# Two recurrent layers ordered one behind the other, and attention stacks written without DRAM

## The reference

```
x = x + attention(cond1(x, f, f))
x = x + ffn(cond2(x, f, f))

cond(r, k, v), for each channel c and batch:
  decay = exp(-exp(w[c])) * (0.5 + 0.5*tf[b]);  ek = exp(min(k,30));  ekv = ek*v
  (nf, df), (nb, db) = a[t] = a[t-1]*decay + (ekv, ek)[t], forward and backward in t
  euk = exp(min(u[c]+k, 30))
  num = nf + nb - ekv + euk*v;   den = df + db - ek + euk
  out = sigmoid(r) * num / max(den, 1e-8) * (0.8 + 0.2*tf[b])
```

## Time and profile before

| | before |
|---|---|
| time, median of 3 runs | 406.08 us (406.03 to 406.85) |
| the profiled execution | 407.77 us, span 405.9 us |
| PE busy | 317.9 us (78%) |
| DVE busy | 322.0 us (79%) |
| ACT busy | 201.4 us (50%) |
| POOL busy | 126.4 us (31%) |
| granted clock, mean | 0.898 of 2.4 GHz |
| data moved by DMA | 55.09 MB |

### The profile page before, as it was taken

How to read it: one execution, slowest core, us unless ns; L and a number is a source line. 1 busy time by engine, 2 the same in 40 slices (tenths; PEclk the granted TensorE clock), 3 DMA queues, 4 the chain that set the end, 5 groups by cost and what they waited for, 6 DMA issues and landing times.

```text
span 405.9 us, 6016 instructions
## 1 busy us (share of the span) xinstructions
PE 317.9 (78%) x1552; PEld 245.0 (60%) x1552; DVE 322.0 (79%) x625; ACT 201.4 (50%) x373; POOL 126.4 (31%) x116
## 2 busy tenths in 40 slices
PE   0042378378858887877897897999999999999994
PEld 0031256165737565555665675888888888888882
DVE  6989888966897475686567995888888988888883
ACT  4131406162625264366555564666666666666651
POOL 1519424162050001001222342334334334334331
PEclk9999559658965896896999998999999999999999
DMA  5965907801760176300543544556655566666531
GB/s 174 169 166 151 155 6 185 129 0 56 155 107 3 52 159 103 106 10 8 170 137 131 154 167 156 140 201 186 189 190 192 183 196 190 192 185 190 194 140 52
DMA packets 33055, 55.09 MB, mean 136 GB/s; under 512 B 5207, under 2 KB 13831, under 8 KB 32011
## 3 DMA queue, kind: packets, MB, share of 16 engines
q1 hardware_dynamic: 33034, 54.85, 50.4%
HBM read 47.55 MB, written 5.52 MB: 131 GB/s over the span
## 4 chain that ended last, share of the span: by engine, by line
PE 48%; DVE 13%; issue 3%; ACT 3%; DMA 2%; POOL 1%; DVEq 0%; SPq 0%; ACTq 0%
PE ps L1256 7%; PE ps L1258 7%; PE ps L1257 6%; PE ps L1267 6%; PE ps L1268 6%; PE ps L1269 6%; PE ps L1171 3%; DVE q_st L959 2%; DVE scan L1052 2%; DVE mx L806 2%; PE ps L1139 2%; DMA k_st<-qk_split 2%; DVE qk_lo L1057 1%; PE ps L1158 1%; PE ps L1128 1%
## 5 line engine op out<-in xcount | busy, mean ns | idle before, releaser
L457 POOL TENSOR_TENSOR scan<-scan 128x512 f32<-128x512 f32 x68 | 73.3, 1078 | 137.8 <-ACT scan L584 136.1
L1057 DVE TENSOR_TENSOR qk_lo<-scan,qk_hi 128x512 fp32r<-128x512 f32 x68 | 69.3, 1019 | 31.7 <-ACT qk_hi L591 31.7
L584 ACT ACTIVATE scan<-ps 128x512 f32<-128x512 f32 x68 | 40.7, 599 | 50.2 <-PE ps L1258 50.0
L1267 PE MATMUL ps<-qk_hi,k_st 128*128 128x512 f32 x136 | 54.5, 401 | 4.5 <-DVE qk_lo L1057 4.3
L1256 PE MATMUL ps<-hid_hi,k_st 128*128 128x512 f32 x136 | 54.6, 401 | 2.0 <-DVE q_st L959 2.0
L577 ACT ACTIVATE k_st<-clip 128x512 fp32r<-128x512 f32 x68 | 42.8, 631 | 24.8 <-PE ps L1269 24.8
L1139 PE MATMUL ps<-k_st,q_st 96*128 96x256 f32 x128 | 34.8, 395 | 25.9 <-DMA k_st<-qk_split 22.6
L1258 PE MATMUL ps<-hid_hi,q_st 128*128 128x512 f32 x136 | 54.1, 398 | 0.0
L1257 PE MATMUL ps<-hid_lo,k_st 128*128 128x512 f32 x136 | 53.9, 396 | 0.0
L1268 PE MATMUL ps<-qk_lo,k_st 128*128 128x512 f32 x136 | 53.5, 393 | 0.0
L1269 PE MATMUL ps<-qk_hi,q_st 128*128 128x512 f32 x136 | 53.5, 393 | 0.0
(11 more groups left out here) (118 smaller groups left out, 461.8 us busy)
## 6 DMA issues: line engine op xcount, KB each, us to landing
clip<-in_tiles SPq DMA_DIRECT2D x68, 256.0 KB, 3.0
ex<-gates SPq DMA_DIRECT2D x136, 128.0 KB, 2.9
q_st<-qk_split SPq DMA_DIRECT2D x16, 256.0 KB, 4.8
k_st<-qk_split SPq DMA_DIRECT2D x32, 128.0 KB, 5.6
qk_split<-qk_hi SPq DMA_DIRECT2D x8, 256.0 KB, 2.2
qk_split<-qk_lo SPq DMA_DIRECT2D x8, 256.0 KB, 2.2
f_sb<-in_fT SPq DMA_DIRECT2D x4, 256.0 KB, 10.5
x_sb<-in_xT SPq DMA_DIRECT2D x4, 256.0 KB, 9.7
```

Of the source, the lines that this page charges most:

```text
L457: g.tensor_tensor(sq[:, k], relu[:, k], relu[:, k], ALU.mult).then_inc(sq_ready, 1)
L1057: TT(act_lo[:, k], act[:, k], act_hi[:, k].bitcast(F32), ALU.subtract).then_inc(act_lo_ready, 1)
L1267: mm(acc, w_hi, act_hi[:, k], start=first, stop=False, skip_group_check=True)
```

## The change

Four things change together.

1. **Stacks.** `qk_dram` and `store_qk` go. `load_stack(b, half)` writes the stack of one half from `qk_hi` and `qk_lo` on chip, with 8 DMAs of 128 KB (16 rows of 8 KB in the stack out of 128 partitions of 1 KB), each pair waiting only for its half of q or k. `MAXROW` goes from 96 to 64: scores contract over 64 rows, shifted scores over 66, and no rows of zeros are filled. `evacuate_qk` waits for the stacks of the batch before to have landed, in place of the stores.
2. **Recurrences.** `scans`, `sums` and `num_den` are called for one layer and one of numerator and denominator at a time. Batch 0 works layer 1 up to hidden1 first, layer 2 between the projections; in the loop, layer 2 of batch b + 1 stands between the first maxima of batch b and layer 1 of batch b + 2 in its second part. For batch 0, POOL makes the sums of layer 2.
3. **Clips and exponentials.** Each exponential waits for its own clip, in the order f, f + u1, x, f + u2. `clips(b + 2)` stands behind the first 8 maxima of batch b, `exponentials(b + 2)` behind `evacuate_o(b - 1, 3)` and ahead of `evacuate_qk(b + 1, 0)`. `products` waits for one exponential at a time.
4. **Loads.** The two small loads `vec` and `cond` are issued by ACT. On SP the loads of x and f of batches 2 and 3, `wo`, `gw` and `gbb` move behind the first stacks; `bvb` behind batch 1. The projection of batch 0 waits for two of the three weight loads, `project_out` for the third. `unity` becomes part of `ones`.

```diff
-MAXROW = 96
+MAXROW = STACK
...
-            def load_stack(w, b, half):
+            def load_stack(b, half):
 
                 n = slot(b, half)
-                sp.wait_ge(st_qk[w], 32 * (b + 1))
                 if turn(b, half) > 1:
                     sp.wait_ge(t_ready, HB * (KC * b + half - SLOTS + 1))
-                src = qk_dram[w, b, half]
-                width = STACK // (2, 4)[w]
-                for r in range(0, STACK, width):
-                    rows = src.rearrange("n d s -> (n d) s") if w == 0 else src[r // (STACK // 2)]
-                    sp.dma_start((q_st, k_st)[w][r:r + width, n].rearrange("p h s -> p (h s)").bitcast(F32),
-                                 rows).then_inc(ld_stack[n], 16)
+                for w in range(2):
+                    for m, (part, ready) in enumerate(((qk_hi, qk_hi_ready), (qk_lo, qk_lo_ready))):
+                        sp.wait_ge(ready, 4 * b + 2 * w + half + 1)
+                        for role in ((m, m + 2), (2 * m, 2 * m + 1))[w]:
+                            sp.dma_start((q_st, k_st)[w][role * HD:(role + 1) * HD, n].bitcast(F32),
+                                         part[:, w, half].bitcast(F32)).then_inc(ld_stack[n], 16)
...
-            store_qk(0)
-            for half in range(KC):
-                for w in range(2):
-                    load_stack(w, 0, half)
+            load_stack(0, 0)
+            load_f(2)
+            load_x(2)
+            load_stack(0, 1)
+            sp.dma_start(wo[:], w_out).then_inc(ld_w, 16)
+            load_f(3)
+            load_x(3)
...
             products(0)
+            sums(0, 1, 1)
+            sums(0, 1, 0)
             products(1)
-            sums(1, 0, 4)
+            sums(1, 0, 1)
+            sums(1, 0, 0)
             add_logs1(1)
             for b in range(B):
+                if b + 1 < B:
+                    sums(b + 1, 1, 1)
+                    sums(b + 1, 1, 0)
                 if b + 2 < B:
                     products(b + 2)
-                    sums(b + 2, 0, 2)
+                    sums(b + 2, 0, 1)
                 if b > 0:
                     add_logs2(b - 1)
                 if b + 2 < B:
-                    sums(b + 2, 2, 4)
+                    sums(b + 2, 0, 0)
...
-                for n in range(4):
+                for i, n in enumerate((0, 1, 3, 2)):
+                    sc.wait_ge(clip_ready, 6 * b + (1, 3, 4, 6)[i])
                     a.activation(ex[:, n], clip[:, n], ACT.Exp, scale=1.0 if n < 3 else -1.0).then_inc(ex_ready, 1)
...
                     evacuate_o(b - 1, 3)
+                if b + 2 < B:
+                    exponentials(b + 2)
                 if b + 1 < B:
                     evacuate_qk(b + 1, 0)
...
-                if b + 3 < B:
-                    exponentials(b + 3)
...
-            scans(0, 0, 0, 4)
-            scans(0, 1, 0, 4)
-            scans(0, 0, 4, 8)
+            scans(0, 0, 1, 0)
+            scans(0, 0, 1, 1)
             first_sums(1)
-            num_den(0, 1)
-            scans(0, 1, 4, 8)
+            scans(0, 0, 0, 0)
+            num_den(0, 0, 1)
+            scans(0, 0, 0, 1)
             first_sums(0)
-            num_den(0, 0)
+            num_den(0, 0, 0)
             first_logs()
             hidden1(0)
+            scans(0, 1, 1, 0)
+            scans(0, 1, 1, 1)
+            dve.wait_ge(ld_w, 32)
+            split_qk(0, 0)
+            scans(0, 1, 0, 0)
+            split_qk(0, 1)
+            scans(0, 1, 0, 1)
+            num_den(0, 1, 1)
+            num_den(0, 1, 0)
             clips(1)
-            scans(1, 0, 0, 8)
-            dve.wait_ge(ld_w, 48)
-            split_qk(0, 0)
-            scans(1, 1, 0, 4)
-            split_qk(0, 1)
-            scans(1, 1, 4, 8)
             add_v_bias(0)
-            num_den(1, 1)
-            clips(2)
-            num_den(1, 0)
+            scans(1, 0, 1, 0)
+            scans(1, 0, 1, 1)
+            scans(1, 0, 0, 0)
+            scans(1, 0, 0, 1)
+            num_den(1, 0, 1)
+            num_den(1, 0, 0)
...
                 for h in range(HB):
                     maximum(b, h)
                     next(route_last, None)
+                    if nxt and h < 4:
+                        scans(b + 1, 1, 1 - h // 2, h % 2)
+                    if nxt and h == 4:
+                        num_den(b + 1, 1, 1)
                     if nxt and h == 5:
                         hidden1(b + 1)
+                    if nxt and h == 6:
+                        num_den(b + 1, 1, 0)
+                if nxt2:
+                    clips(b + 2)
                 low_max(b, 0)
...
                 if nxt2:
-                    scans(b + 2, 1, 0, 6)
+                    num_den(b + 2, 0, 1)
+                    scans(b + 2, 0, 0, 1)
                 if b > 0:
                     hidden2(b - 1)
                 if nxt2:
-                    scans(b + 2, 1, 6, 8)
-                    num_den(b + 2, 1)
-                    num_den(b + 2, 0)
-                if b + 3 < B:
-                    clips(b + 3)
+                    num_den(b + 2, 0, 0)
```

More of the change, by code:

```diff
@@ L264, in _, with load_f, load_x @@
         def _(sp):
-            sp.dma_start(vec[:], vecs).then_inc(ld_vec, 16)
-            sp.dma_start(cond_sb[:], cond.partition_broadcast(P)).then_inc(ld_vec, 16)
-            for b in range(B):
+            def load_f(b):
                 sp.dma_start(f_sb[:, :, tok(b)], fT[:, :, tok(b)]).then_inc(ld_f[b], 16)
+            def load_x(b):
                 sp.dma_start(x_sb[:, :, tok(b)], xT[:, :, tok(b)]).then_inc(ld_x[b], 16)
[L270 to L282, removed]
+            load_f(0)
+            load_x(0)
+            sp.dma_start(wi[:], w_in).then_inc(ld_w, 16)
+            load_f(1)
+            load_x(1)
+            sp.dma_start(bvb[:], bv.partition_broadcast(P)).then_inc(ld_w, 16)
+            sp.wait_ge(ones_ready, 1)
+            sp.dma_start(k_st[MAXROW:MAXROW + 2].rearrange("p n h s -> p (n h) s").bitcast(F32),
+                         ones[0:2].unsqueeze(1).broadcast_to([2, SLOTS * HB, S])).then_inc(ld_ones, 16)
             def load_raw(t, k):
@@ L342, in _ @@
                 if b + 1 < B:
-                    store_qk(b + 1)
-                    for w in range(2):
-                        load_stack(w, b + 1, 0)
+                    load_stack(b + 1, 0)
                 if b + 1 == B:
@@ L353, in _ @@
                 if b + 1 < B:
-                    for w in range(2):
-                        load_stack(w, b + 1, 1)
-            sp.wait_ge(st_unity, 16)
+                    load_stack(b + 1, 1)
+            sp.wait_ge(st_ones, 16)
             sp.wait_ge(lnsum1_ready, B)
@@ L399, in products, with sums @@
                 pool.wait_ge(ld_f[b], 16)
-                pool.wait_ge(ex_ready, 4 * b + 3)
                 if b > 0:
                     pool.wait_ge(bwd_ready, 8 * b)
+                pool.wait_ge(ex_ready, 4 * b + 1)
                 g.tensor_tensor(ekv[:], ex[:, 0], f, ALU.mult).then_inc(pool_pre, 1)
                 for n in range(2):
+                    pool.wait_ge(ex_ready, 4 * b + (2, 4)[n])
                     g.tensor_tensor(gk[:, n], gk[:, n], ex[:, 0], ALU.subtract).then_inc(pool_pre, 1)
-                for n in range(2):
-                    pool.wait_ge(pool_pre, 5 * b + 2 + n)
+                    pool.wait_ge(pool_pre, 5 * b + 2 * n + 2)
                     g.tensor_tensor(gkv[:, n], gk[:, n], f, ALU.mult).then_inc(pool_pre, 1)
[L410 to L414, removed]
-                        pool.wait_ge(pool_pre, 5 * b + 2 + n)
-                        pool.wait_ge(fwd_ready, 8 * b + 2 * n + 2)
-                        row, term = 2 + n, gk
-                    else:
-                        pool.wait_ge(pool_pre, 5 * b + 4 + n)
-                        pool.wait_ge(fwd_ready, 8 * b + 4 + 2 * n + 2)
-                        row, term = n, gkv
-                    g.tensor_tensor(scan[:, row], scan[:, row], term[:, n], ALU.add).then_inc(esum_ready, 1)
+            def sums(b, n, which):
+                pool.wait_ge(pool_pre, 5 * b + 2 * n + (3, 2)[which])
+                pool.wait_ge(fwd_ready, 8 * b + 4 * n + (4, 2)[which])
+                row = 2 * which + n
+                g.tensor_tensor(scan[:, row], scan[:, row], (gkv, gk)[which][:, n], ALU.add).then_inc(esum_ready, 1)
             def add_logs1(b):
@@ L499, in evacuate_qk @@
                 if b > 0:
-                    sc.wait_ge(st_qk[w], 32 * b)
+                    for half in range(KC):
+                        sc.wait_ge(ld_stack[slot(b - 1, half)], 128 * turn(b - 1, half))
                 job = ("qk"[w], b)
@@ L720, in _, with scans @@
             clips(0)
-            def scans(b, back, first, last):
-                for i in range(first, last):
-                    which, n, c = 1 - i // 4, i // 2 % 2, i % 2
-                    if i == 0 and not back:
+            def scans(b, n, which, back):
+                if not back:
+                    if b == 0 and n == 0 and which == 1:
```

(8 more changed lines are left out.)

80 lines of the change are left out of this document (36 added, 44 removed).

## The result

| | before | after |
|---|---|---|
| median of 4 runs | 406.47 us (406.03 to 407.31) | 426.1 us (424.5 to 427.7) |
| ratio, 95% interval | | 1.0497 (1.0433 to 1.0561) |
| profiled execution, span | 407.77, 405.9 us | 424.84, 423.0 us |
| granted clock, mean | 0.898 | 0.85 |

What follows compares the result with a forecast made beforehand. DVE was taken to bound batches 0 and 1, PE, ACT and the stacks batches 2 and 3. 8.8 - 0.6 - 6.8 + 1.5 + 0.4 = 3.3 us gained, from 406.08 to 402.8; range 396.5 to 408.

Steps and rivals of the forecast that it cites:

- A rule against the change: Around the scores: a shape switch costs 0.16, at most 0.36 us; by the skill's rule 64 and 66 rows differ in mode.
- rival 2: 64-row scores pay a switch to and from 66 or 128 rows, 5 to 11 us, about 410; chance 0.12.
- The start: Before batch 0's first maximum: layer 1 goes first to hidden1, first maximum at 39.0 against 47.8, 8.8 us gained.
- The stacks' landing: Stack DMAs behind the k projection: the last 0.5 MB lands some 4.5 us behind k_lo, against 10.3 before.
- Rival 4: Stack DMAs slower than the DRAM route, needing over 11 us for 0.5 MB: 408; chance 0.04.
- Batches 0 and 1: DVE work per batch conserved: batch 0 again 33.3 us, batch 1 net +0.6, bounds 3.2 and -2.2.
- Batch 2's payback: First part of batch 2: batch 3's second layer now lies there, 6.8 us longer, bounds 5.0 and 8.
- Before batch 3: The 3.4 us stack wait goes and hidden2(1) is late next: 1.5 us gained, plus 0.4 for the clock.
- Rival 3: Batch 2's payback and batch 1's ACT order eat all, 8 for 6.8, hidden2(1) late as before: 406; chance 0.12.
- Rival 1: The start's gain survives as DVE and POOL may collide less in batches 0 to 2: about 397; chance 0.20.

Runs made afterwards that it cites:

- experiment 2: The changed kernel with one row of zeros in both stacks, so scores contract over 65 rows instead of 64: 418.08 us, ratio 1.03.
- experiment 5: The kernel before with stacks written on chip, old order, at 64, 65, 96 and 126 rows: 419.81, 410.48, 402.3 and 401.44 us.
- experiment 3: The changed kernel with 96 rows, 32 of them zeros, instead of 64: 409.12 us, ratio 1.0078.
- experiment 6: The changed kernel with 96 rows, and vec and cond issued first on SP again: 407.35 us, ratio 1.0102.
- experiment 9: Experiment 8's kernel with ACT's exponentials(b + 2) behind evacuate_qk(b + 1, 0) and DVE's first scans behind split_qk and normalise: 402.41 us, ratio 0.9916.
- Experiment 8: Experiment 6's kernel with the last batch's layer 2 moved from between batch 2's first maxima into its later part: 403.93 us, ratio 0.9972.
- kernel 4: The kernel before, old order and 96 rows, with stacks written on chip instead of going through DRAM: 402.3 us, ratio 0.995.

## Why the prediction was wrong

**The step that failed is "A rule against the change" and rival 2 with it.** I saw rows that priced a switch, 0.16 us and at most 0.36, though one of another kind (32 columns to 128), and the 0.36 has no working; between 64 and 66 rows it measures 0.20 at full clock and 0.30 at half. I saw where it would decide, about 30 times in batches 2 and 3. I gave it 0.12 all the same, with "nothing in the diff but the row count asks for it". That is no argument: the row count was in the diff. No row of the trace could decide whether 64 and 66 rows switch, since 96 and 98 don't; with the question open and a price at which the sign turned (0.11 a switch) it had to weigh near even. The Trainium skill (TensorEngine Tiling (Array Packing), Tiling Modes, Key Properties) says that a change of the tiling mode drains the engine; by that rule the trace agrees, with 0.43 us a pair for 0.23 and 7 to 9 us of the total by experiments 2 and 5. No run names a mode, though; what the runs show is the price.

**Rival 2 was itself mis-sized, by the clock.** It priced the drain alone, about 410. 30 switches of 0.20 to 0.30 are 6 to 9 us; from 64 to 65 rows experiments 2 and 5 measured 8.0 and 9.3 by the medians (8.0 and 7.1 by the ratios). What it lacked is a second term as large: 65 to 96 rows, 9.0 us in the new order and 8.2 in the old (9.0 and 10.2 by the ratios), with the granted clock up from 0.69 to 0.77 and from 0.72 to 0.80. No step of the prediction had a clock that could fall with the number of rows. The rows to ask were there: the clock stood at 0.74 and 0.82 in batches 2 and 3 and fell to 0.50 in places, so this stretch lay between the two levels, and PE set its pace. I had taken that as a gain of 0.4 us. That the clock carries this term rests on pairs that are equally far apart at equal clock with 65 and 96 rows; why rows of zeros raise it no run here shows.

The sum of both terms is 17 us from experiments 2 and 3 together (426.1 to 409.1); from 64 to 96 rows in experiment 5 it is 17.5. It leaves 6 us of my error of 23 to the other steps:

- **The start: 8.8 us forecast, 3.4 measured, and the 5.4 us lacking are nearly all of those 6.** 1.9 are cond, whose DMA I took as unchanged because "the moved x, weight and constant loads lie beside this"; it was the one load on the path, and moved to another queue it landed 2 us later (experiment 6). Another 1.7 lies ahead of hidden1's end and is DVE beside POOL: the clips took 2.7 us (8.11 to 10.84) where I had 1.8, and the clamp 1.37 where I had 0.38. 0.3 lies between hidden1's end and k_lo: I had 7.3, it took 7.6 (21.64 to 29.2, the end of k_lo's first half, the first of the two at 28.79). The last 1.5 lies behind k_lo, where one addition took 1.68 us in place of 0.68 beside POOL's, with 0.7 idle ahead of it.
- **The stacks' landing** was forecast 4.5 us behind k_lo and took about 8 (29.2 to 37.42). SP issued each pair in 1.25 us, and the DMAs took 3.9 to 6.2 us to land, by the page's medians. It cost nothing: DVE came to the first maximum 7 us later, as I had argued. Rival 4, whose harm began at 11 us, did not come.
- **Batches 0 and 1:** the first took 33.2 (forecast 33.3). The second took 40.2 with 64 rows and 40.3 with 96: +1.5 and +1.6 over the earlier trace rows for a forecast of +0.6, inside the bounds. Part of it was the wait behind the exponentials that I had named: experiment 9 took 2 us of it away.
- **Batch 2's payback: right.** +6.8 forecast for the first part. From the first maximum to the eighth it took 14.8 us with 96 rows in experiment 3 and 16.1 in 6, and 8.4 to 8.5 in the old order: +6.3 to +7.7. Experiment 8 took this work out and 3.4 us came back in the median.
- **Before batch 3: right in kind.** The stack's wait is gone, hidden2 is what PE waits for. Alone, in the old order, it is worth 2 to 4 us, against 1.5 + 0.4 in my sum. From the eighth maximum on, batch 2 took 23.0 us in kernel 4, at a granted 1.00, and 27.2 before, at 0.81. Only a part of this is the pause's: before, 1.2 GHz lasted for 7.4 us, to 135.6, ahead of the pause, and again from 152.6, within the pause, for the last 2.8 us of the batch. The second piece is the term that I had put at 0.4; the first I had not foreseen, and no run shows why it is shorter with stacks on chip.
- With 96 rows the stretches of batches 0, 1 and 2 stood within 1 us of the forecast (32.1, 40.3, 40.1 us against 33, 39.5 and 40), and batch 3 within 1.3 (38.9 against 40.2): the order was costed well, and a start good for 3.4 us cannot pay for a batch 2 that costs 6.4. So even with 96 rows the change is slower (1.0078), and this part of the sign hung on the start.

Rival 3, that payback and ACT's order eat all, comes near the time with 96 rows (409 against its 406), but its mechanism holds in part alone: the payback was not the 8 us that it needed in experiment 3, and what was lacking most was the start. Rival 1 fell: POOL and DVE did not collide less.

## What to carry to other kernels

Look at the row counts of matmuls that alternate: here 64 beside 66 cost 7 to 9 us of 406, one row of zeros (65 beside 67) mended it, and 96 rows gave 8 to 10 us more, with a higher granted clock. Rows of zeros that look like waste are to be tried with and without before they are removed. A suspicion that only a rule supports and the trace can't refute deserves at least even odds when the diff steps right onto it. A gain at the start that is paid for by moving work into a stretch where DVE is full must be larger than that work, and a small load that stands at the head of the path is to be followed whenever its queue changes.

## What was not expected of the hardware

- With the same instructions on every engine and the same switches, 65 rows ran at a granted 0.72 and 96 rows at 0.80 (batch 3 alone: 0.66 and 0.83); 126 rows gave no more, 0.80. The additional rows were zeros.
- A load of cond on ACT's queue, issued at 1.16 us, reached its reader at 6.22; on SP's queue ahead of the loads of f and x, issued at 1.20, at 4.27. Whether the queue or the loads issued beside it did this was not tried apart.
- A DMA of 128 KB from 128 partitions into 16 took a median 3.9 to 6.2 us from issue to landing, in the order in which eight of them were issued:

```profile
q_st<-qk_hi SPq DMA_DIRECT2D x16, 128.0 KB, 3.9
...
k_st<-qk_lo SPq DMA_DIRECT2D x16, 128.0 KB, 6.2
```
